# A fused attention and mixture-of-experts kernel: one block instead of two, early slots on GpSimd, another order at the start and in the late routing

## What is computed

```python
q = rope(x @ Wq.T); k = rope(x @ Wk.T); v = x @ Wv.T        # 16 query heads, 4 key/value heads of 128
attn = softmax(causal(q @ k.T / sqrt(128)))                 # per batch and head
x = layernorm(x + (attn @ v) @ Wo.T)
scores = softmax(x @ gate_w.T)                              # 64 experts
topk_w, topk_ids = top_k(scores, 6); topk_w /= sum(topk_w) + 1e-20
routed = sum over the 6 experts of topk_w * ((silu(g_e(x)) * u_e(x)) @ w_down_e)   # width 176
shared = (silu(sg(x)) * su(x)) @ ws_down                    # width 352
out = layernorm(x + routed + shared)
```

## Time and profile before

| what | us |
|---|---|
| median of 3 runs (lowest, highest) | 1334.73 (1334.47, 1335.14) |
| the profiled execution | 1332.91 |
| its span, first to last instruction | 1331.1 |
| PE busy | 1227.7 (92%) |
| DVE busy | 1023.2 (77%) |
| ACT busy | 859.0 (65%) |
| GpSimd (POOL) busy | 790.4 (59%) |
| PE clock granted, mean over the span | 0.977 |

### The profile page before, as it was taken

How to read it: one execution, slowest core, us unless ns; L and a number is a source line. 1 busy time by engine, 2 the same in 40 slices (tenths; PEclk the granted TensorE clock), 3 DMA queues, 4 the chain that set the end, 5 groups by cost and what they waited for, 6 DMA issues and landing times. The chain is left out here.

```text
span 1331.1 us, 28521 instructions
## 1 busy us (share of the span) xinstructions
PE 1227.7 (92%) x8636; PEld 1105.6 (83%) x8636; DVE 1023.2 (77%) x2162; ACT 859.0 (65%) x1973; POOL 790.4 (59%) x796
## 2 busy tenths in 40 slices
PE   5899999999999999989999998997969999999967
PEld 3799889889889889878888886886859999999955
DVE  2677777677677777878877887886837999999946
ACT  3665666666576666656666565676227999988932
POOL 5654744654584464365456445443775888888852
PEclk7999999999999999999999999998989999999979
DMA  7766765776558785676577567750357888888857
GB/s 249 204 184 164 187 184 154 186 201 172 147 127 209 212 212 141 164 191 171 162 185 205 136 174 204 187 139 20 95 168 218 259 266 260 255 267 262 263 217 309
DMA packets 196601, 256.51 MB, mean 193 GB/s; under 512 B 13642, under 2 KB 167678, under 8 KB 196500
## 3 DMA queue, kind: packets, MB, share of 16 engines
q1 hardware_dynamic: 183332, 227.85, 61.7%
q0 software_dynamic: 11040, 25.30, 5.7%
q10 hardware_dynamic: 2128, 2.10, 0.5%
HBM read 90.43 MB, written 169.72 MB: 195 GB/s over the span
## 5 line engine op out<-in xcount | busy, mean ns | idle before, releaser
L846 DVE TENSOR_REDUCE neg_max<-scores 128x1 f32<-128x256 f32 (+7 forms) x256 | 192.2, 751 | 152.1 <-PE scores L969 151.4
L608 ACT ACTIVATE pt_hi<-pt 128x512 fp32r<-128x512 f32 (+3 forms) x384 | 174.7, 490 | 188.1 <-PE pt L978 186.1
L581 ACT ACTIVATE probs<-scores,neg_max 128x256 f32<-128x256 f32 (+7 forms) x256 | 189.8, 742 | 48.4 <-DVE neg_max L846 48.3
L802 DVE TENSOR_TENSOR pt_lo<-pt,pt_hi 128x512 fp32r<-128x512 f32 (+3 forms) x384 | 200.3, 549 | 22.7 <-ACT pt_hi L608 21.0
L871 PE MATMUL o_ps<-pt_hi,v_hi 128*128 128x256 f32 (+1 forms) x640 | 193.7, 303 | 8.7 <-DVE o_lo L810 8.5
L872 PE MATMUL o_ps<-pt_lo,v_hi 128*128 128x256 f32 (+1 forms) x640 | 180.0, 281 | 0.0
L873 PE MATMUL o_ps<-pt_hi,v_lo 128*128 128x256 f32 (+1 forms) x640 | 179.6, 281 | 0.0
L978 PE MATMUL pt<-ident,probs 128*128 128x128 f32 x1152 | 169.6, 274 | 6.2 <-DVE pt_lo L802 6.2
L538 POOL TENSOR_TENSOR turned<-turned,turn_sin 128x512 f32<-128x512 f32 x80 | 105.5, 1318 | 114.5 <-DVE turn_sin L784 59.3
L1291 POOL DMA_INDIRECT results_dram<-rows,dest x134 | 145.1, 1083 | 33.1 <-issue 26.4
L969 PE MATMUL scores<-k_hi,q_lo 128*128 128x512 f32 (+4 forms) x384 | 151.8, 395 | 0.0
(11 more groups left out here) (280 smaller groups left out, 3680.3 us busy)
## 6 DMA issues: line engine op xcount, KB each, us to landing
rows_dram<-empty SPq DMA_DIRECT2D x256, 524.1 KB
up_raw<-in_up SPq DMA_DIRECT2D x69, 368.0 KB
xt<-rows_dram SPq DMA_DIRECT2D x68, 258.0 KB, 2.7
rows<-results_dram SPq DMA_DIRECT2D x16, 768.0 KB, 12.7
down_raw<-in_down SPq DMA_DIRECT2D x69, 128.0 KB
down_raw<-in_down_tail SPq DMA_DIRECT2D x69, 112.0 KB
w_raw<-in_w SPq DMA_DIRECT2D x8, 768.0 KB, 6.9
wo_raw<-in_wo SPq DMA_DIRECT2D x8, 512.0 KB, 9.5
```

What stands on the lines that cost most here:

```text
L581: nc.scalar.activation(probs[:, at_probs(k, m), 0:w], scores_ps[m % 2][:, score_cols(m)], ACT.Exp, bias=neg_max[:, m % 4:m % 4 + 1], accum ...
L608: nc.scalar.activation(pt_hi[m // 2 % 2][:, a:z, P * (m % 2):P * (m % 2) + P], pt_ps[c % 2][:, 0:P * (z - a)].rearrange("p (k q) -> p k q" ...
L802: nc.vector.tensor_tensor(pt_lo[m // 2 % 2][part], pt_ps[c % 2][:, 0:P * (z - a)].rearrange("p (k q) -> p k q", q=P), pt_hi[m // 2 % 2][pa ...
L846: nc.vector.tensor_reduce(neg_max[:, n % 4:n % 4 + 1], scores_ps[n % 2][:, score_cols(n)], AX.X, ALU.max, negate=True).then_inc(max_made, 1)
```

## The change

There are four parts. First, one block for both functions: semaphores of attention live on, and in place of the block's end each engine calls `attention_over`. Second, the opening: KV columns of the first weights in a DMA of their own, T two steps after K, and DVE makes the upper cosine half and the addition for the first K and the first Q. Third, slots of the early groups go from EARLY_DVE to a function `slot` on GpSimd; the six comparisons are kept from the masks (`chosen`) instead of being made again, and the reduction is six halvings. Fourth, the late part: `logits(0)` before turn 0, turns 6 and 7 and `logits(1)` behind two shared units and turns 1 to 3; DVE makes two of the norms of group 1, then the chain of group 0 to `notes(0)`, then the other two norms and shared_hide(0); places(0) moves to the bank of the logits. ACT's order follows.

```diff
+OPENING = {STEPS + FILLS["T"][0]: ("K", len(FILLS["K"])), STEPS + FILLS["T"][0] + 2: ("T", len(FILLS["T"])),
+           STEPS + FILLS["K"][0]: None}
...
-             (2, 43): [(0, "slot", 0)], (2, 47): [(0, "slot", 1)], (2, 50): [(0, "slot", 2)],
-             (2, 51): [(0, "slot", 3), (0, "slot", 4)], (2, 53): [(0, "slot", 5)], (2, 54): [(0, "slot", 6)],
-             (2, 55): [(0, "slot", 7), (0, "slot", 8)], (2, 57): [(0, "slot", 9)], (2, 58): [(0, "slot", 10)],
-             (2, 59): [(0, "slot", 11), (1, "norm", 0)], (2, 61): [(1, "norm", 1)], (2, 62): [(1, "norm", 2)],
+             (2, 59): [(1, "norm", 0)], (2, 61): [(1, "norm", 1)], (2, 62): [(1, "norm", 2)],
...
+EARLY_SLOT = {(2, 48): (0, 0), (2, 50): (0, 1), (2, 52): (0, 2), (2, 54): (0, 3), (2, 56): (0, 4), (2, 58): (0, 5),
+              (3, 34): (1, 0), (3, 46): (1, 1), (3, 50): (1, 2), (3, 52): (1, 3), (3, 54): (1, 4), (3, 58): (1, 5)}
...
-    if first and n in (STEPS + FILLS["T"][0], STEPS + FILLS["K"][0]):
-        return ("K" if n == STEPS + FILLS["T"][0] else "T"), len(FILLS["K"])
+    if first and n in OPENING:
+        return OPENING[n]
...
+                        cols = slice(0, WCOLS)
+                        if first and i == SPLITS:
+                            sp.dma_start(w_raw[:, :, KV_COLS], dram["w"][bass.ds(kv_at(i), 1), :, :, KV_COLS]
+                                         .rearrange("o p k c -> (o p) k c")).then_inc(first_in, 16)
+                            cols = Q_COLS
...
+            def slot(g, j):
+                tiles = slice(GT * g, GT * (g + 1))
+                pool.wait_ge(mask_made, g + 1)
+                pool.wait_ge(slot_of_made, g + 1)
+                pool.wait_ge(weights_made, g + 1)
+                done_steps = E.bit_length() * (g * TOPK + j)
+                pool.tensor_tensor(at_slot, chosen[j], slot_of, ALU.mult).then_inc(slot_step, 1)
+                pool.wait_ge(slot_step, done_steps + 1)
+                for halving in range(E.bit_length() - 1):
+                    some = E >> (halving + 1)
+                    pool.tensor_tensor(at_slot[:, :, 0:some], at_slot[:, :, 0:some], at_slot[:, :, some:2 * some],
+                                       ALU.add).then_inc(slot_step, 1)
+                    pool.wait_ge(slot_step, done_steps + 2 + halving)
+                pool.tensor_copy(slots_int[:, tiles, j], at_slot[:, :, 0]).then_inc(slots_made, 1)
+                pool.wait_ge(slots_made, g * TOPK + j + 1)
...
                             nc.gpsimd.tensor_tensor(turned[r % 2][0:64], taken[r % 2][64:128], cos[64:128, pos], ALU.mult).then_inc(cos_made, 1)
+                            if opens(first, *use):
+                                made["turn"] += 1
+                                continue
...
+                    if early_at(EARLY_SLOT, k, n) is not None:
+                        slot(*early_at(EARLY_SLOT, k, n))
...
-                    then(dve.tensor_tensor(picked[:] if i > 0 else mask[:], expert_ids[:].unsqueeze(1).broadcast_to([P, GT, E]),
+                    then(dve.tensor_tensor(chosen[i], expert_ids[:].unsqueeze(1).broadcast_to([P, GT, E]),
...
-                if part == "slot":
...
+            def turn_upper(k, kind, i):
+                r = rope_of(kind, i)
+                pos = slice(half(kind, i) * HALF, (half(kind, i) + 1) * HALF)
+                nc.vector.tensor_tensor(turned[r % 2][64:128], taken[r % 2][0:64], cos[0:64, pos], ALU.mult).then_inc(cos_made, 1)
+                dve.wait_ge(cos_made, 2 * now(k, len(ROPES), r + 1))
+                dve.wait_ge(sin_made, now(k, len(ROPES), r + 1))
+                nc.vector.tensor_tensor(turned[r % 2][:], turned[r % 2][:], turn_sin[r % 2][:], ALU.add).then_inc(turn_made, 1)
...
+        def attention_over(eng):
+            for b in range(RING_ROWS):
+                eng.wait_ge(rows_sent[b], 16 * SENDS // RING_ROWS)
+            for g in range(GROUPS):
+                eng.wait_ge(empty_out[g], 16 * EMPTY_DMAS // GROUPS)
+            eng.wait_ge(resid_added, now(ROUNDS - 1, per("O"), per("O")))
...
-        places_ps = [first_places_ps[:, 0:GT * E], counts_ps[:, E:E + GT * E]]
+        places_ps = [logits_ps[0][:, GT * E:2 * GT * E], counts_ps[:, E:E + GT * E]]
...
             turn_taken(0)
             fill_rows(0)
-            turn_taken(6)
-            turn_taken(7)
-            shared_silu_of(0)
             fill_rows(2)
             exps(0)
+            shared_silu_of(0)
             shared_silu_of(1)
-            for j in range(1, 4):
+            for j in (1, 2, 3, 6, 7):
                 turn_taken(j)
...
-            norms(1)
+            norms(1, 0)
             dve.wait_ge(consts_set, 1)
             tops(0)
             ids(0)
-            shared_hide(0)
             choices(0)
             masks(0)
-            tops(1)
             weights(0)
             places(0)
             slot(0, 0)
             notes(0)
+            norms(1, 1)
+            shared_hide(0)
             slot(0, 1)
             shared_hide(1)
+            slot(0, 2)
+            tops(1)
             ids(1)
-            slot(0, 2)
             choices(1)
...
             late_turn(5)
+            logits(0)
             late_turn(0)
-            logits(0)
-            late_turn(6)
-            late_turn(7)
             pe.wait_ge(shared_in, 48)
             shared_gate_up(0)
-            logits(1)
             shared_gate_up(1)
             places(0)
-            for j in range(1, 4):
+            for j in (1, 2, 3, 6, 7):
                 late_turn(j)
+            logits(1)
             shared_gate_up(2)
...
-        attention(nc, dram, resid, consts)
-        feed_forward(nc, dram, resid, consts, out)
+        block = ctx.enter_context(nc.Block())
+        attention_over = attention(nc, dram, resid, consts, block, ctx)
+        feed_forward(nc, dram, resid, consts, out, block, attention_over)
```

More of the change, by code:

```diff
@@ L250, in run_rounds, with attention @@
     body(ROUNDS - 1, False, True)
-def attention(nc, dram, resid, consts):
+def attention(nc, dram, resid, consts, block, semaphores):
     with ExitStack() as ctx:
@@ L357, in exchanged, with opens @@
             return k + i // per(kind) < EXCHANGED_ROUNDS
+        def opens(first, kind, i):
+            return first and i == per(kind)
         def turned_into(kind, i):
@@ L507, in body @@
                     if use and use[0] in "KQ" and runs(use[1], per(use[0]), first, last):
-                        if not (first and n < STEPS):
+                        if not opens(first, *use):
                             turn_low(pool, nc.gpsimd, k, *use)
@@ L626, in body @@
                     if runs(i, SPLITS, first, last):
+                        if first and i == SPLITS:
+                            act.wait_ge(first_in, 16)
+                            nc.scalar.activation(w_hi[0][:, :, KV_COLS], w_raw[:, :, KV_COLS], ACT.Copy).then_inc(first_hi_made, 1)
                         act.wait_ge(w_in, 16 * (SPLITS * k + i + 1))
@@ L792, in body @@
                     low = fill_at(n - 3, first)
-                    if first and n < STEPS and low and low[0] in "KQ" and runs(low[1], per(low[0]), first, last):
+                    if low and low[0] in "KQ" and opens(first, *low):
                         turn_low(dve, nc.vector, k, *low)
@@ L814, in body @@
                         turn_by_sine(k, *turn)
+                        if opens(first, *turn):
+                            turn_upper(k, *turn)
                     q = (n - 5) // 4
```

81 lines of the change are left out of this document (42 added, 39 removed).

## The result

The changed kernel takes 1320.93 us (median of 4 runs, 1319.71 to 1322.91) beside 1334.93 us for the kernel before on the same chip: a ratio of 0.9893, 95% interval 0.9874 to 0.9912. That is 14.0 us, where 15.2 were forecast. The profiled execution took 1322.91 us, its span is 1320.9: 10.2 us less than the span of before.

What follows compares the result with a forecast made beforehand. TensorE, busy 92% of the span, was taken as the bound, so its waits counted. Terms 4.6 + 4.0 + 2.6 + 4.0 = 15.2 us took 1334.73 to 1319.5 us, range 1312 to 1328.

Steps and rivals of the forecast that it cites:

- 1. Opening: Kernel start: split first load, T two steps after K and a divided turn save 4.6 us, ends 2.5 and 6.
- copy at about 13.1, Q at about 13.6: Opening: ACT reaches T's copy before k_hi, so the Q product starts 3.7 us earlier.
- two halves run on two engines: Opening: DVE's upper cosine half (0.69 us) runs beside GpSimd's lower half, making Q's turn some 1.8 us shorter.
- 2. Slots: Attention rounds 2 and 3: moving 12 early slots from DVE to GpSimd saves 4.0 us, between 0 and 9.5.
- DVE is not relieved: Rival, 20%: GpSimd's small reads hold DVE up, or ACT and clock caused the excess; slots give 0 to -4 us.
- 3. One block: Seam between attention and late routing: dropping the barrier between blocks saves 2.6 us, ends 1.8 and 3.2.
- the first late send 4 us closer: Confirming sign, late routing: the first row send comes 4 us closer to attention's last addition than the present 23.2 us.
- 4. Late routing: Chain from the seam to GpSimd's row sends: reordering starts the sends sooner, saving 4.0 us, ends 3.0 and 5.0.
- places wait for both shared units on PE: Late routing: two units at 2.6 us end at 920.0, masks at 920.5, so the wait is hidden, 0.5 us spare.
- slower rival: Rival, 5%: GpSimd falls over 11 us behind its turns, PE waits for q_lo, slots cost full length: 1363 us.

Runs made afterwards that it cites:

- busy and copy later: Changed kernel plus 11 large dummy TensorE products around attention's end, GpSimd's first row copy held behind two late norms: 1365.21 us, ratio 0.9940 on the slower chip.
- busy: Changed kernel plus the dummy TensorE products around attention's end, GpSimd's row copy left where the changed kernel has it: 1320.69 us, ratio 0.9895.
- v_lo first: Changed kernel with VectorE making the first V's v_lo ahead of the first Q's upper cosine half and sum: 1365.33 us, ratio 0.9935 on the slower chip.
- 38 dummies: Changed kernel plus 38 unread products of a constant on TensorE ahead of the first real product: 1362.53 us, ratio 0.9908 on the slower chip.
- all three edits: Changed kernel plus early dummy products, v_lo ahead of Q's upper half, and dummies around attention's end with GpSimd's copy behind two norms: 1315.23 us, ratio 0.9859.

## Why the prediction was right, and where it was not

The traces side by side give the opening. The second and third columns are the start of the first product of V and of Q and the distance of their products in us; the fourth is the time at which the profile first records the full clock, the last the row maximum of (1,0).

| kernel | V starts, apart | Q starts, apart | clock up | (1,0) |
|---|---|---|---|---|
| before | 11.55, 0.23 | 17.29, 0.23, then 0.43 | 11.2 | 235.5 |
| old opening | 11.55, 0.23 | 17.30, 0.23, then 0.43 | 11.3 | 235.4 |
| slots back | 11.39, 0.22 | 13.72, 0.23 | 11.3 | 231.9 |
| late order undone | 11.45, 0.23 | 13.79, 0.24 | 10.8 | 230.9 |
| changed, three traces | 11.2 to 11.4, 0.43 | 14.9 to 15.0, 0.43 | 18.4 to 30.9 | 234.2 to 234.8 |
| busy and copy later, busy | 11.38, 0.43 | 14.99, 0.43 | 25.7, 26.5 | 235.0, 235.4 |
| two blocks | 11.71, 0.43 | 15.33, 0.43 | 31.2 | 234.7 |
| whole turn on GpSimd | 11.50, 0.43 | 15.12, 0.23 | 15.2 | 232.6 |
| v_lo first | 11.41, 0.43 | 15.03, 0.43 | 24.3 | 233.7 |
| 38 dummies | 10.27, 0.24 | 12.61, 0.24 | 7.9 | 231.1 |
| all three edits | 9.91, 0.23 | 12.24, 0.24 | 6.1 | 229.2 |

**1. Opening: right in kind, mis-sized.** The term "copy at about 13.1, Q at about 13.6" holds to 0.2 us where TensorE's clock is up in time (13.72 and 13.79), and then 3.6 to 4.5 us arrive at (1,0), my 4.6, with first scores at 21.6 and 22.5 us. Where it isn't, V and Q take 2.5 us more and 0.1 to 1.2 us arrive. I had taken V's 0.23 us distance from the trace of before without asking whether it would be there again. Code that is the same up to V's products sees the full clock anywhere between 10.8 and 31.2 us, so this looks left to the execution. That the run times of one kernel fall into groups some 4 us apart (the late order undone: 1320.03 and 1320.16, then 1324.21 to 1326.22) fits, and the profiled run of the fast group has the fast opening. It isn't shown for each run, since only one execution of each kernel has a trace. The Trainium skill (TensorE: Matmul & The Clock Gate, What's actually happening) says that TensorE rests at the lower level and rises after activity, and that the number of slow products differs between runs of one kernel. The table agrees, and the dummies confirm the first half. The second mis-sized term is the upper cosine half, "two halves run on two engines": 1.64 us beside GpSimd's instead of the 0.69 that I gave it. Q's turn still became shorter, from 5.3 us (20.35 to 25.67) to 3.1 (18.59 to 21.64), but v_lo stood behind it, and PE behind v_lo.

**2. Slots: right, or a little better.** 5.5 us for 4.0 in the first pair of traces. In all twelve traces with slots on GpSimd this part takes 649.4 to 651.0 us, and before it took 654.9: 3.9 to 5.5. The four that have two stretches of half clock in it, like the kernel before, give 3.9 to 4.4. Cost of a slot 3.2 us for 3.3, no wait of PE for GpSimd's q_lo, the late sends 0.30 us apart as before. The rival "DVE is not relieved" had its mechanism right, but 3.2 us of contention stand against 23.2 of work. By the rule of the Trainium skill (SBUF — State Buffer, Who interferes with whom) that I cited there, this part would have been 0. The opening's rows agree with the rule: beside GpSimd's half DVE's takes 1.64 us and ends 0.55 us behind it, alone 0.69. What the rule would do here was mis-sized: GpSimd's new operations last 0.2 to 0.7 us each, and all of them together cost the 57 sine products 3.2 us. The stretch of half clock at 594.9 us of before, up to 1.7 us, belongs to what the slots cost, as the experiment showed; I had put a lower clock in round 2 beside them, as something else. The steps that I called 35 to 56 run to the row maximum of step 57.

**3. One block: right.** 2.7 us for 2.6; PE 0.95 us behind the last addition, where I had 0.9. One sign of mine contradicts my sum: "the first late send 4 us closer" to the last addition than 23.2 us, where terms 3 and 4 together make 6.6. It came 19.2 us behind, 4.0 closer. So the sign came true only because term 4 failed.

**4. Late routing: right in kind, mis-sized.** 1.3 us for 4.0. The step that failed is "places wait for both shared units on PE: 914.8 + 2 x 2.6 = 920.0 ... Hidden, 0.5 to spare". The 2.6 us for a unit were at full clock; at half clock the first took 5.3 (3.75 for its first group of products and 1.91 for its tail, overlapping), logits 3.67 for 2.24, and DVE waited 2.72 us. With the clock kept up the same chain takes 14.6 to 15.0 us, 4.5 to 5 less than before: more than my 4.0, the excess being the clock that the kernel before did not have either. That the send loop sets the end held: 61.8 us from first to last send, and the routed part 334.9 us long against 334.7.

So the total came out close by luck: in the profiled pair one term was too small and two too large and 10.2 us are left of 15.2, and the median probably holds runs with the better opening, which the one trace for each kernel can't show. The slower rival never came near: GpSimd wasn't late for q_lo once.

## What to carry to other kernels

Removing a wait from TensorE's path pays by the clock that it meets there. Where an engine goes straight from waiting into a critical chain, read the start distance of its products before and behind the wait, and price the chain at both levels. Dummy products in the time in which it would stand idle anyway, 38 small and 11 large ones, cost 0.2 to 0.5 us and gave 2.3 to 3.3 us in two places of this kernel by the traces. Splitting one elementwise pass over DVE and GpSimd at the same moment gained nothing here, as each slowed the other and the next pass stood behind both; small pieces of other work on GpSimd did pay.

## What was not expected of the hardware

- **The granted clock has a blind spot.** For 12 to 16 us the changed kernel's windows say 1.00, and the products of that stretch start 0.427 us apart. The profile has no clock record before 18.4 us there. At the start of this kernel only the distance of products tells.
- **Short waits inside attention were followed by half clock.** The changed kernel had 3.4 us of it at 694.3 us, others at 591.5, 704.2, 813.4. PE was nearly full before, but just ahead of each of these it had waited 1.9 to 2.3 us for DVE, so such a wait cost more than its own length:

```profile
693.76 0.39 PE L908 MATMUL proj_ps<-wo_hi,o_hi 128*128 128x256 f32 x1 [1.98 <-DVE resid L867]
```

A wait of 1.98 us at 810.9 in the same trace was not followed by it.
- **One chip was 3% slower, in one place.** Attention ended at 900.3 us against 899.1. But the sends took 68.3 us for 61.8, the routed part began 33 us behind them instead of 6, and it lasted 348.5 us for 334.9. Between 930 and 951 us PE has pauses before single products with nothing to wait for, and from 932.0 us on 23.9 us of half clock, which the traces of the other chips don't have there:

```profile
937.55 0.21 PE L1861 MATMUL counts_ps<-mask,ones 128*128 128x64 bf16 x1 [0.49 <-issue]
938.96 0.58 PE L1819 MATMUL shared_gate_up<-xt,w_raw 128*128 128x256 f32 x1 [1.19 <-issue]
940.36 1.50 PE L1819 MATMUL shared_gate_up<-xt,w_raw 128*128 128x256 f32 x2 [0.81 <-issue]
```

All four kernels of that set show the long wait ahead of the routed part, the kernel before took 1374 us there too, and the cause stays open. Ratios on that chip are to be compared with each other only.
